# Two Swin blocks on one core: the normalisation subtracts the mean as bn_aggr leaves it, without an instruction that negates it

## The reference

```python
def _layernorm(x, g, b, eps=1e-05):
    mu = x.mean(-1, keepdims=True)
    var = ((x - mu) ** 2).mean(-1, keepdims=True)
    return (x - mu) * jax.lax.rsqrt(var + eps) * g + b
...
def swin_block(x, gamma1, beta1, w_qkv, b_qkv, w_proj, b_proj, gamma2, beta2, w_fc1, b_fc1, w_fc2, b_fc2):
    x = x.transpose(0, 2, 3, 1)
    shortcut = x
    x = layer_norm(x, gamma1, beta1)
    x = jnp.roll(x, shift=(-SHIFT[0], -SHIFT[1]), axis=(1, 2))
    x = window_attention(x, w_qkv, b_qkv, w_proj, b_proj)
    x = jnp.roll(x, shift=(SHIFT[0], SHIFT[1]), axis=(1, 2))
    x = shortcut + x
    shortcut = x
    x = layer_norm(x, gamma2, beta2)
    x = jax.nn.gelu(x @ w_fc1 + b_fc1, approximate=False) @ w_fc2 + b_fc2
    x = shortcut + x
    return x.transpose(0, 3, 1, 2)
```

## Time and profile before

| | |
|---|---|
| median of 3 runs | 4314.11 us (4303.97 to 4317.73) |
| profiled execution | 4314.22 us, its span 4312.3 us |
| TensorE busy | 4027.5 us, 93% of the span |
| VectorE busy | 3364.9 us, 78% |
| GpSimd busy | 3062.7 us, 71% |
| ScalarE busy | 2709.6 us, 63% |
| granted TensorE clock | 0.999 of full speed |

### The profile page before, as it was taken

The page is one execution under the profiler, slowest core; times in us unless marked ns, Lnnn a source line. Parts: engine busy times, 40 slices in busy tenths (PEclk is TensorE's granted clock), DMA queues, the critical chain, the costliest instruction groups (busy, mean ns, idle before and its releaser), DMA issues. The chain is left out here.

```text
span 4312.3 us, 175439 instructions
## 1 busy us (share of the span) xinstructions
PE 4027.5 (93%) x66384; PEld 2912.2 (68%) x66384; DVE 3364.9 (78%) x9085; ACT 2709.6 (63%) x5921; POOL 3062.7 (71%) x6257
## 2 busy tenths in 40 slices
PE   4999999999999999999999999999999999999998
PEld 2666667667766666776676677667667766766665
DVE  6887777778778777787777778787777778777785
ACT  1666666666666666666666666666666666666665
POOL 4777777777777777777777777777777777777664
PEclk9999999999999999999999999999999999999999
DMA  4655556556565655555555555556555655565553
GB/s 98 104 96 100 98 95 99 102 95 99 104 98 97 100 102 92 103 100 96 98 100 98 97 99 102 97 97 101 102 91 101 100 97 98 100 101 96 90 95 61
DMA packets 1544449, 420.50 MB, mean 98 GB/s; under 512 B 1441334, under 2 KB 1542074, under 8 KB 1543612
## 3 DMA queue, kind: packets, MB, share of 16 engines
q1 hardware_dynamic: 1543612, 409.29, 54.9%
HBM read 31.56 MB, written 25.17 MB: 13 GB/s over the span
## 5 line engine op out<-in xcount | busy, mean ns | idle before, releaser
L573 PE MATMUL ps_s<-xh,w_fc 128*128 128x512 f16 x3840 | 909.7, 380 | 60.7 <-ACT stage L687 47.6
L941 DVE TENSOR_TENSOR hid<-scaled,hid 128x512 f16<-128x512 f32 x768 | 597.9, 779 | 449.7 <-POOL hid L1109 430.7
L1047 POOL TENSOR_TENSOR rstd<-vare,half 128x2 f32<-128x2 f32 x520 | 361.2, 695 | 801.5 <-DVE vare L881 801.5
L586 PE MATMUL bank<-w_fc,hid 128*128 128x192 f16 x9216 | 847.7, 246 | 77.7 <-DVE hid L941 71.9
L586 PEld LDWEIGHTS bank<-w_fc,hid 128*128 128x128 f16 x9216 | 764.6, 98 | 156.7 <-DVE v_blk L897 80.6
L573 PEld LDWEIGHTS ps_s<-xh,w_fc 128*128 128x128 f16 x3840 | 335.3, 97 | 621.0 <-ACT scaled L701 217.5
L1109 POOL TENSOR_SCALAR hid<-scaled 128x512 f16<-128x512 f32 x768 | 609.4, 794 | 182.8 <-ACT scaled L701 182.2
L701 ACT ACTIVATE scaled<-ps_s,b_fc 128x512 f32<-128x512 f32 x768 | 529.3, 690 | 308.9 <-DVE hid L941 306.8
L693 ACT ACTIVATE pt<-ps_t 128x768 f16<-128x768 f32 x512 | 415.3, 811 | 324.0 <-PE ps_t L530 316.8
L666 ACT ACTIVATE xs<-xn 128x192 f16<-128x192 f32 x512 | 184.6, 361 | 579.0 <-POOL xn L1053 579.0
L449 PE MATMUL bank<-w_qkv,xh 128*128 128x384 f16 x2560 | 500.9, 326 | 6.2 <-DMA xh<-xs 3.6
(11 more groups left out here) (113 smaller groups left out, 7341.9 us busy)
## 6 DMA issues: line engine op xcount, KB each, us to landing
x_img<-in_x_dram SPq DMA_DIRECT2D x256, 96.0 KB, 2.2
out_dram<-y_img SPq DMA_DIRECT2D x256, 96.0 KB, 1.9
xh<-xs SPq DMA_TRANSPOSE x520, 2.8
qkt<-qk SPq DMA_TRANSPOSE x512, 4.0
ot<-os SPq DMA_TRANSPOSE x512, 2.3
stage<-in_L_conv_fc_w_dram SPq DMA_DIRECT2D x2, 384.0 KB, 4.3
stage<-in_L_conv_w_fc_dram SPq DMA_DIRECT2D x2, 384.0 KB, 4.0
stage<-in_L_conv_qkv_w_dram SPq DMA_DIRECT2D x2, 288.0 KB
```

Source lines behind the costliest of these rows:

```text
L573: last = mm(ps_s[:, u % 2, :].rearrange("p (a t) -> p a t", a=GROUP), w_fc1[layer][:, part, m * 128:(m + 1) * 128], xh[:, p % 2 * GROUP:(p ...
L586: mm(bank[:, 0:C], hid16[:, hs, m, tok], w_fc2[layer][:, ws, m, :], start=(m == 0 and i == 0), stop=False)
L941: v.tensor_tensor(hid16[:, 1, m, :], hid[:, u % 2, :], hid16[:, 0, m, :], ALU.subtract)\
```

## The change

`nmean` and the instruction that writes it go. GpSimd's normalisation reads the mean from `mv` as bn_aggr leaves it, and subtracts it where it added the negative. Since `mv` is now read until the normalisations are done, bn_aggr waits for those of the visit two before, which used the same buffer; `centre` waits for the `rstd` of two before instead.

```diff
-        nmean = sb("nmean", [128, 2, 2], F32)
...
                 def mean_variance(n, which):
                     a = "12"[which]
                     ge(f"bn{a}a", n)
+                    ge(f"ln{a}", n - 2)
+                    if which == 0:
+                        ge("hi1", n - 2)
                     dve.nop(nofuse=True)
                     v.bn_aggr(mv[:, n % 2, which, :], bn6[:, which, n % 2, :]).then_inc(S["bn" + a], 1)
...
                         ge("bn2", m - 8)
-                    ge("hi1", m - 2)
-                    ge("ln1", m - 2)
-                    ge("ln2", m - 10)
+                    ge("rstd", m - 2)
                     dve.nop(nofuse=True)
-                    v.tensor_scalar(nmean[:, r, :], mv[:, r, :, 0], -1.0, None, ALU.mult)
                     v.tensor_scalar(vare[:, r, :], mv[:, r, :, 1], EPS, None, ALU.add).then_inc(S["centred"], 1)
...
-                    g_.tensor_scalar(dst, stream(n, which), nmean[:, r, which:which + 1], rstd[:, r, which:which + 1],
-                                     ALU.add, ALU.mult).then_inc(S[done], 1)
+                    g_.tensor_scalar(dst, stream(n, which), mv[:, r, which, 0:1], rstd[:, r, which:which + 1],
+                                     ALU.subtract, ALU.mult).then_inc(S[done], 1)
```

## The result

The changed kernel takes 4619.23 us (median of 4 runs, 4609.89 to 4621.74) against 4315.15 us of the kernel before (4 runs): ratio 1.0703, 95% interval 1.0684 to 1.0722. It was forecast at 4305 us. It is 304 us slower.

A forecast was written before the change was run, and what follows sets the result against it. The prediction took a chain in each phase's first half, headed by nmean and vare, to bound the kernel: 4314.2 us less 9.0 less 0.4 gives 4304.8, say 4305 us; range 4294 to 4318.

The forecast's parts named there:

- What bounds the kernel: In a phase of four slots, the first half is set by a chain without slack; in the second TensorE is full.
- chain of place 0: In a phase's first slot, vare to the last low part of the hidden layer, 12.84 us, with nmean in front.
- second half: Second MLP product to the next phase's first scores: TensorE busy 17.04 of 17.04 us, which VectorE or GpSimd cannot shorten.
- nmean goes, 9.4 us: Head of the first slot's chain: vare ends 0.07 us earlier, 9.0 us in 128 phases, plus 0.4 us outside them.
- margin of 0.21 us: Second high part of the hidden layer: without the low part beside it, it would end 0.21 us earlier, given ScalarE's activation.
- The waits, nothing: Moved waits at the aggregations and vare: nothing waits, cost nil.
- cover that was read as 7.1 us: Before an aggregation: the normalisations of the tile two before ended 7.1 us earlier, so the moved wait costs nothing.
- GpSimd subtracts the mean: GpSimd's three normalisations: subtraction taken at the addition's 0.50 us; upper bound 0.55 us each, 19 us in all.
- dearer-subtraction rival: Normalisations behind rstd in a phase's first slot take 0.05 us more each: +10 us, 4324 us; chance 0.07.
- In the three slots that are not the first of a phase ... worth nothing there: Time saved there lies beside a TensorE that is never idle, or behind the last low part: no gain.
- Placement: Tiles behind nmean move down by 32 bytes; no row prices it, taken as nothing.

The follow-up runs named there:

- hi0_ahead: The kernel before with vare written ahead of nmean, and the hidden layer's first high part ahead of the slot's last normalisation on GpSimd in place 0; 4319.94 us.
- after: The changed kernel itself, against the kernel before; 4619.23 us, ratio 1.0703.
- sub_only: The kernel before with nmean holding the mean in its own sign and GpSimd subtracting it; no instruction, wait or tile moved; 4650.44 us, ratio 1.0776.
- sub_place0: The kernel before with the mean in its own sign and GpSimd's subtraction in slots of place 0 alone, addition elsewhere; 4540.81 us, ratio 1.0519.

## Why the prediction was wrong

*What bounds the kernel*: right. The chain of place 0 stands in every kernel of the table, and so does the second half; a gain of 0.07 us at the head comes out as 0.07 us of the phase. The second half was read from one phase: it is not full in all, as said above, but no kernel makes it shorter or longer in the median.

*nmean goes, 9.4 us*: right in mechanism and nearly in size. add_in_place, which is the change without its subtraction, is 17 us faster (11 to 22), 9.5 us of it on the predicted way. It came out at 4298 us where the sum gave 4305; the 7 us between are not explained by the mechanism. The margin of 0.21 us that the second high part has up to ScalarE was not tested by any kernel: in hi0_ahead ScalarE held the first high part, and the slow normalisation the second.

*The waits, nothing*: right; one idle of 1.7 us in all, under a cover that was read as 7.1 us.

*GpSimd subtracts the mean*: here it failed. The step said "Upper: the subtraction of two tensors of the same size, 0.55 us (553 ns)", and took 0.50. The row is another instruction, so it bounded nothing: the tensor-scalar with a subtraction takes 1.01 us. The dearer-subtraction rival had the right place and the right sum but a price of 0.05 us: with 0.51 its own arithmetic, 3 by 0.51 by 128 less 9, gives 187 us, and lacks place 3 and the clock. For an operation without a row of its own, the range should have stayed open upwards.

*"In the three slots that are not the first of a phase ... worth nothing there"*: right for a gain, wrong for a loss of this size. In place 3, 1.5 us more of GpSimd run past their cover. The prediction never measured that cover, since it asked only which engine waits, not by how much the third normalisation could slip until ScalarE's next instructions and GpSimd's own power are late. ScalarE's high part (L666) was already waiting for it before the change (1.52 us, at 2002.66 above); what had room was what stands behind it. That is 91 us. The other 224 us are place 0: 1.53 us in the chain and 0.18 in the ladder (high and low parts in turn), where two high parts now stand back to back in front of the first low part, which takes 1.02 us for 0.69. By medians 128 by 1.71 = 219; by means 207, and the rest is the clock, a cost that the prediction did not have.

*Placement*: taken as nothing; no cost shows, as add_in_place has the moved tiles and is not slower for them.

## What to carry to other kernels

An operation that seems free to exchange (add for subtract, with the sign kept elsewhere) has a price of its own on GpSimd: keep tensor-scalars there to pairs that have a row in a trace (add with mult in either order or mult with mult here, not add with add), and put the sign into an instruction that VectorE executes anyway. An instruction in front of another at the head of a chain costs about the distance of their starts (0.07 to 0.08 us here), so changing the order of the two gives what removing one gives. And ask of each engine not only whether it waits, but how far each of its results may slip before another queue stands: the same half microsecond, three times in a slot, cost 224 us in place 0, 91 in place 3 and 2 in places 1 and 2 together. Where a longer chain leaves TensorE idle, look at the granted clock too: some 19 of the 304 us came by it.

## What the runs showed that was not expected

GpSimd's tensor-scalar has two speeds. For 128x192 elements with add, mult (operands from memory) 0.50 us, with subtract, mult 1.01; with immediates mult, add 0.35 us against 0.87 for subtract, mult and 0.86 for max, mult. Add with add belongs to the slow ones (128x48: 0.39 against 0.23 us), mult with mult to the fast. In hi0_ahead, where a low part of VectorE (two inputs in SBUF) and a normalisation of GpSimd that started 0.12 us earlier ran together, it was GpSimd's that took twice its time (1.02 for 0.50 us), and VectorE's that took its usual 0.69. The Trainium skill, SBUF — State Buffer, Who interferes with whom, says that whichever issues first gets the shared ports and the other blocks. By the starts in this trace it was the other way here; the trace shows starts and not issues, and the spans of GpSimd may be off by a little.

TensorE's clock fell to half with the subtraction in place 0: 21, 26 and 18 stretches in after, sub_only and sub_place0, whose mean granted clock is 0.991 to 0.993 in the profiled executions; 1 to 5 stretches in all other kernels, at 0.998 or more. Of the four runs of the changed kernel the one with the highest clock (0.995) is also the fastest (4609.89 us).
